# A decoder layer with 18 experts: rates and weights asked for earlier, two experts' products ahead, and the expert loops written out

## The chip, the cores and the metric

The kernel runs on one core of a Trainium2 chip. The core has five engines that run their own instruction streams and meet only at semaphores: TensorE (PE in the profile, matrix products), VectorE (DVE), ScalarE (ACT), GpSimd (POOL), and SyncE (SP), which here only issues DMAs. PSUM is eight banks of 128 x 512 floats; every product of TensorE lands there. The metric is the device time of one execution in microseconds (us), the median of several runs.

## What is computed

One decoder layer on `x` of 4 x 256 tokens with 256 features: a gated linear attention of 16 heads, a mixing of tokens by a softmax over a context, and an expert layer. Each has a layer norm ahead of it and is added to `x`. The change is in the second and the third.

```python
# mixing by context (query, key are bilinear maps of ctx_1024)
energy = einsum('bnd,bmd->bnm', query, key)
attention = softmax(energy, axis=-1)
x_m = einsum('bln,bmn->blm', x_norm, attention)
# experts: 2 shared (always used, weight 1) and 16 routed, 4 of them chosen per token
scores = sigmoid(hidden @ gate_weight.T)
#   two of four groups by their two best scores, then the four best experts, rates scaled to 2.5
y = sum over experts of  rate * ((silu(x @ gw.T) * (x @ uw.T)) @ dw.T)
```

## The kernel before, in words

All is one function, `decoder_layer`, with one instruction stream per engine, written by hand; the order of the work is the order of the code, and semaphore waits (`wait_ge`) hold an engine until another has got far enough. Every product of full precision is made of three (`mm3`, lines L1258 to L1260): both operands are split in a high and a low half, and high x low, low x high and high x high are added in PSUM. The high half is a copy on ScalarE, the low half a subtraction on VectorE or GpSimd.

The 16 heads fill the first 390 us and are not touched. Then comes a stretch in which the last head's output, the context softmax and the norms follow each other: ScalarE makes exponentials (`context_exp`, L685), scales them (`context_soft`, L693) and copies transposed tiles (`context_att`, `half_out`); VectorE adds into `x`, takes statistics and runs a chain of some 14 small operations for the norm's factors (`norm_factors`, L851 to L891); TensorE transposes (`half_transpose`, L1269) and mixes (`mix`, L1254). All of it goes in two halves of 512 tokens, `c` = 0 and 1.

The expert part has these pieces, `n` counting experts from 1 (1 and 2 are the shared ones, 3 to 18 the routed ones):
- `router_logits(c)` on TensorE, a sigmoid on ScalarE, a transpose, and then on VectorE a chain from L1179 to L1238 that chooses experts and makes the rates (`weight`, inside the tile `obet`). TensorE transposes the rates (L1646), ScalarE copies them, SP writes them to DRAM as rows (`route_rows`) and loads a row back for each expert, spread over all partitions (`load_route`, into `wbc`, the tile `tap`).
- `gate_up(n)` on TensorE: gate and up products of both halves, 24 matmuls of 512 columns into `e_ring` (banks 0 to 3).
- `gate_silu` (ScalarE, L777), `u_times` (VectorE, product of silu and up, L1149, into `prod`, the tile `conv`), `weigh` (GpSimd, times the rates, L502, into `act_w`, the tile `gate`), `act_high` (ScalarE, L786), `act_low` (VectorE, L1158): these make the two halves of the expert's activations.
- `down(n)` on TensorE: 24 matmuls of 256 columns, added up over all experts in `y_acc` (banks 4 to 7).
- Weights: SP loads 384 KB per expert into one of two slots of `w_raw`; ScalarE copies the high half (`gate_up_high` L761, `down_high` L768), GpSimd makes the low half (`gate_up_low` L484, `down_low` L490).

In before, TensorE multiplies one expert ahead: `gate_up(n + 1)` stands ahead of `down(n)`. The tiles of an expert's activations exist once. The shared experts are weighted on GpSimd too, by ones set with a memset (L508). Experts 5 to 18 run in a hardware loop of seven rounds of two on each engine (`Fori`).

Of the kernel before, what the change touches and what calls it, by code (L numbers as in the profile page):

```python
# [126 lines left out]
def decoder_layer(nc, x_in, ctx_in, xw_in, xb_in, wb_in, bb_in, w_in, prm_in, wv_in, wo_in,  # L127
# [5 lines left out]
    with ctx:  # L133
# [83 lines left out]
        mix_acc = bank[6:8] + bank[4:6]  # L217
        energy = (bank[0], bank[1], bank[0], bank[6])
# [10 lines left out]
        ld_w = [sem(f"ld_w{i}") for i in range(2)]  # L229
        ld_prm = [sem(f"ld_prm{i}") for i in range(G)]  # L230
# [29 lines left out]
        ones_ready = sem("ones_ready")  # L260
# [9 lines left out]
        def _(sp):  # L270
# [90 lines left out]
            def expert_split(n):  # L361


                sp.wait_ge(down_lo_ready, n - E_SHARED)


# [5 lines left out]
            load_expert(4, 1)  # L372
            sp.wait_ge(r_tr_ready, NCH)
# [3 lines left out]
            def load_route(e, s, before):  # L377

                sp.wait_ge(e_weighted, before)
# [17 lines left out]
        def _(pool):  # L397
# [89 lines left out]
            def down_low(n, s):  # L487
                w = slice(s * 3 * D + 2 * D, (s + 1) * 3 * D)
                pool.wait_ge(down_hi_ready, n - E_SHARED)
# [3 lines left out]
            def weigh(n, s, first):  # L493

                for c in range(NCH):
                    pool.wait_ge(u_prod, (n - 1) * NCH + c + 1)
                    if not first:

                        pool.wait_ge(e_hi, (n - 2) * NCH + c + 1)
                        pool.wait_ge(e_lo, (n - 2) * NCH + c + 1)  # L500
                    cc = slice(c * N, (c + 1) * N)
                    nc.gpsimd.tensor_tensor(act_w[:, cc], prod[:, cc], wbc[:, s * T + c * N:s * T + (c + 1) * N],  # L502
                                            ALU.mult).then_inc(e_weighted, 1)

            pool.wait_ge(p_added, TT // 2)
# [1211 lines left out]
```

## Time and profile before

| | |
|---|---|
| median of 3 runs | 598.84 us (596.99 to 599.95) |
| the profiled execution | 597.41 us |
| its span, first to last instruction | 595.5 us |
| PE busy | 557.4 us, 94% of the span |
| DVE / ACT / POOL busy | 437.1 / 398.3 / 298.9 us |
| chain that ended last | PE 83%, DVE 8%, ACT 4%, DMA 2% |

The span is shorter than the execution's own time by what lies ahead of the first and behind the last instruction. Matmuls overlap in the trace: a matmul of 512 columns is shown with some 0.39 us, but the next begins 0.23 us after it, so lengths of work on PE are taken from start to start. "Idle before" in a row is the time without work of that engine ahead of it, with the engine that ended it.

### The profile page before, as it was taken

How to read it: one execution, taken by the hardware profiler on the slowest of the kernel's cores; microseconds unless marked ns; L12 is line 12 of the kernel's file. 1: busy time of each engine (PE TensorE's matmuls, PEld its weight loads, DVE VectorE, ACT ScalarE, POOL GpSimd, SP SyncE). 2: the span in 40 equal slices, each digit the busy share in tenths (PEclk: the TensorE clock that was granted, in tenths of full speed). 3: DMA queues.
4: the chain of work that ended last, by engine and by line, in shares of the span. 5: the costliest groups of instructions: out<-in, count | busy, mean ns of one | idle time of the engine just before them, and what ended most of it. 6: DMA issues, size and time to landing. Idle time of an engine off the chain costs nothing.

```text
span 595.5 us, 10331 instructions
## 1 busy us (share of the span) xinstructions
PE 557.4 (94%) x3392; PEld 488.2 (82%) x3392; DVE 437.1 (73%) x1046; ACT 398.3 (67%) x783; POOL 298.9 (50%) x201
## 2 busy tenths in 40 slices
PE   3899999999999999999999999897777799999996
PEld 1687889989989989989989988786566688888885
DVE  8778989989989988998998998968593433333334
ACT  4978988878978979879779778665531433343331
POOL 2434756746746646656666563301041655556542
PEclk9998999999999999999999999999998899999999
DMA  6122032032032032032031020110002433333311
GB/s 206 29 107 81 0 117 81 1 116 81 2 117 81 2 116 81 2 116 75 8 116 56 27 97 23 59 29 1 0 1 70 149 105 107 104 123 113 108 62 70
DMA packets 16267, 42.23 MB, mean 71 GB/s; under 512 B 4544, under 2 KB 4800, under 8 KB 16224
## 3 DMA queue, kind: packets, MB, share of 16 engines
q1 hardware_dynamic: 16224, 41.69, 20.9%
q8 instruction: 23, 0.38, 0.3%
q14 instruction: 20, 0.16, 0.1%
HBM read 40.47 MB, written 1.21 MB: 70 GB/s over the span
## 4 chain that ended last, share of the span: by engine, by line
PE 83%; DVE 8%; ACT 4%; DMA 2%; issue 2%; SPq 1%; ACTq 0%; DVEq 0%
PE bank L1258 20%; PE bank L1260 19%; PE bank L1259 19%; PE bank L1254 15%; PE bank L1396 5%; PE bank L1384 4%; ACT tok L624 2%; DMA xbias<-in_xb 1%; DMA w_raw<-in_w 1%; DVE stats L976 1%; DVE xT_lo L911 1%; DVE gated_lo L1158 1%; ACT values L538 0%; DVE x L1248 0%; DVE raw L995 0%
## 5 line engine op out<-in xcount | busy, mean ns | idle before, releaser
L1258 PE MATMUL bank<-xT_lo,w_hi 128*128 128x512 f32 x336 | 140.0, 417 | 3.6 <-DVE conv L1149 1.3
L1260 PE MATMUL bank<-xT_hi,w_hi 128*128 128x512 f32 x336 | 132.3, 394 | 0.0
L1259 PE MATMUL bank<-xT_hi,w_lo 128*128 128x512 f32 x336 | 131.8, 392 | 0.0
L425 POOL TENSOR_TENSOR gated_lo<-gated,gated_hi 128x512 fp32r<-128x512 f32 x30 | 38.7, 1290 | 116.5 <-ACT gated_hi L644 112.8
L624 ACT ACTIVATE tok<-bank,nmr,rstd 128x128 f32<-128x128 f32 x256 | 91.0, 504 | 2.1 <-DVE nmr L891 2.1
L502 POOL TENSOR_TENSOR gate<-conv,tap 128x512 f32<-128x512 f32 x36 | 46.4, 1291 | 84.5 <-DVE conv L1149 71.4
L1258 PEld LDWEIGHTS bank<-xT_lo,w_hi 128*128 128x128 f32 x336 | 63.5, 189 | 18.8 <-DVE conv L995 3.2
L1260 PEld LDWEIGHTS bank<-xT_hi,w_hi 128*128 128x128 f32 x336 | 63.3, 188 | 14.2
L420 POOL TENSOR_TENSOR conv<-tap,conv 128x506 f32<-128x506 f32 x32 | 61.9, 1934 | 21.8 <-DVE conv L995 21.8
L420 POOL TENSOR_TENSOR raw<-tap,raw 128x506 f32<-128x506 f32 x32 | 61.9, 1934 | 20.3 <-DVE raw L995 16.3
L1259 PEld LDWEIGHTS bank<-xT_hi,w_lo 128*128 128x128 f32 x336 | 63.7, 190 | 9.6
L976 DVE BATCH_NORM_STATS2 stats<-bank 128x6 f32<-128x128 f32 x256 | 56.4, 283 | 16.3 <-PE bank L1384 16.3
L1149 DVE TENSOR_TENSOR conv<-bank,tok 128x512 f32<-128x512 f32 x36 | 24.8, 691 | 50.9 <-PE bank L1260 42.0
L967 DVE TENSOR_TENSOR_SCAN decay<-obet,dmask 128x1536 f32<-128x1536 f32 x16 | 61.9, 3868 | 0.0
L1158 DVE TENSOR_TENSOR gated_lo<-gate,gated_hi 128x512 fp32r<-128x512 f32 x36 | 25.5, 750 | 46.6 <-ACT gated_hi L786 46.6
L636 ACT ACTIVATE qk<-bank,prm 128x512 f32<-128x512 f32 x64 | 51.3, 840 | 0.0
L995 DVE SCALAR_TENSOR_TENSOR raw<-bank,prm,raw 128x510 f32<-128x510 f32 x64 | 46.8, 742 | 5.6 <-ACT tap L592 4.4
L1258 PE MATMUL bank<-w_lo,gated_hi 128*128 128x256 f32 x144 | 42.0, 292 | 9.3 <-DVE gated_lo L1158 9.3
L1254 PE MATMUL bank<-qk 128*128 128x256 f32 (+1 forms) x256 | 50.2, 329 | 0.5 <-DVE x L1028 0.3
L995 DVE SCALAR_TENSOR_TENSOR conv<-bank,prm,conv 128x510 f32<-128x510 f32 x64 | 46.8, 743 | 3.4 <-ACT tap L592 2.2
L1254 PEld LDWEIGHTS bank<-qk 128*128 128x128 f32 x256 | 43.3, 190 | 5.6 <-issue 0.7
L1254 PE MATMUL bank<-probs,values 128*128 128x256 f32 (+1 forms) x256 | 47.0, 327 | 0.0
(167 smaller groups left out, 1358.3 us busy)
## 6 DMA issues: line engine op xcount, KB each, us to landing
w_raw<-in_w SPq DMA_DIRECT2D x34, 384.0 KB, 4.4
obet<-obet_rows SPq DMA_DIRECT2D x16, 768.0 KB, 4.2
tap<-route_rows SPq DMA_DIRECT2D x16, 512.0 KB, 3.6
wv_raw<-in_wv SPq DMA_DIRECT2D x8, 256.0 KB, 4.8
wo_raw<-in_wo SPq DMA_DIRECT2D x8, 256.0 KB, 4.9
x<-in_x SPq DMA_DIRECT2D x2, 512.0 KB, 4.6
out_x<-x SPq DMA_DIRECT2D x4, 256.0 KB, 2.4
raw<-in_ctx SPq DMA_DIRECT2D x1, 512.0 KB, 5.4
```

Source lines behind the costliest of these rows:

```text
L420: nc.gpsimd.tensor_tensor(y, r, y, ALU.add).then_inc(conv_done, 1)
L425: nc.gpsimd.tensor_tensor(gated_lo[:, cc], gated[:, c * N:(c + 1) * N], gated_hi[:, cc].bitcast(F32), ALU.subtract).then_inc(gated_lo_read ...
L502: nc.gpsimd.tensor_tensor(act_w[:, cc], prod[:, cc], wbc[:, s * T + c * N:s * T + (c + 1) * N], ALU.mult).then_inc(e_weighted, 1)
L624: ins = nc.scalar.activation(tok[:, t * P:(t + 1) * P], t_ring[u][:, i * P:(i + 1) * P], ACT.Identity, scale=rstd[:, t:t + 1], bias=nmr[:, ...
L636: nc.scalar.activation(qk[:, u * N:(u + 1) * N], t_ring[u][:, :], ACT.Identity, scale=prm[:, o:o + 1], bias=prm[:, o + 1:o + 2]).then_inc( ...
L967: nc.vector.tensor_tensor_scan(decay[:, :], obet[:, :], dmask[:, :], 0.0, ALU.mult, ALU.add).then_inc(decay_ready, 1)
L976: ins = nc.vector.bn_stats(stats[:, 6 * t:6 * t + 6], t_ring[u][:, i * P:(i + 1) * P])
L995: ins = nc.vector.scalar_tensor_tensor(out=y, in0=r, scalar=prm[:, o + 3 - back:o + 4 - back], in1=y, op0=ALU.mult, op1=ALU.add)
L1254: return nc.tensor.matmul(o, l, r, start=start, stop=stop)
L1258: nc.tensor.matmul(o, l_hi, r_lo, start=start, stop=False, skip_group_check=loose)
L1259: nc.tensor.matmul(o, l_lo, r_hi, start=False, stop=False, skip_group_check=loose)
L1260: return nc.tensor.matmul(o, l_hi, r_hi, start=False, stop=stop, skip_group_check=loose)
```

## The change

Nothing is computed otherwise but this: the shared experts are no longer multiplied by ones. The rest moves work or gives it room:
- Weights of experts 3 and 4 are split early, whole, into the tiles of the attention's weights (`early`: `wv_hi`/`wv_lo`, `wo_hi`/`wo_lo`), which are free by then; ScalarE does it ahead of the second `context_soft`, GpSimd after the first mixed quarter is added to `x`.
- Every tile on an expert's way exists twice (`two`, `weighted`), so TensorE multiplies two experts ahead: `gate_up(n + 2)` ahead of `down(n)`.
- Shared expert 2's first half uses banks 6 and 7 (`e_bank`); the two shared experts are interleaved by halves and parts (`e_count` gives their order). `mix`, norm and router are reordered at this place: the transposes of the router's first half come after three of four mixed quarters, and the second pair of exponentials after the first `half_out`.
- Weight loads are split in gate and up (256 KB) and down (128 KB), and rows of rates are asked for an expert earlier.
- GpSimd makes the next gate weights' low half between its two weightings.
- The loops on all five engines are written out.

```diff
-        act_w = gate
-        act_hi, act_lo = gated_hi[:, 0:T], gated_lo[:, 0:T]
+        act_hi, act_lo = gated_hi[:, 0:2 * T], gated_lo[:, 0:2 * T]
...
+        def two(n, c):
+            return slice(n % 2 * T + c * N, n % 2 * T + (c + 1) * N)
+        def e_bank(n, c, j):
+            return bank[6 + j] if isinstance(n, int) and n == 2 and c == 0 else e_ring[2 * c + j]
+        def e_count(n, c):
+            if isinstance(n, int) and n <= E_SHARED:
+                return n + E_SHARED * c
+            return n * NCH + (c + 1 - NCH)
+        def weighted(n, c):
+            if n <= E_SHARED:
+                return prod[:, two(n, c)]
+            o = n % 2 * 3 * T + c * N
+            return gate[:, o:o + N]
+        def early(n):
+            return (wv_hi[:, 64:64 + 3 * D], wv_lo[:, 64:64 + 3 * D]) if n == 3 else (
+                wo_hi[:, 0:3 * D], wo_lo[:, 0:3 * D])
...
-        mix_acc = bank[6:8] + bank[4:6]
-        energy = (bank[0], bank[1], bank[0], bank[6])
+        mix_acc = bank[4:8]
+        energy = (bank[0], bank[1], bank[6], bank[7])
```

SyncE:

```diff
-            for s in range(2):
-                load_route(s, s, NCH * (s + 1))
-            with sp.Fori(0, E_ROUTED // 2 - 1) as r:
+            for e in range(3):
+                load_route(e, e % 2)
+            for r in range(E_ROUTED // 2 - 2):
                 for s in range(2):
-                    expert_split(r * 2 + (3 + s))
-                    load_expert(r * 2 + (5 + s), s)
-                    load_route(r * 2 + (2 + s), s, r * (2 * NCH) + NCH * (3 + s))
+                    load_gate_up(r * 2 + (7 + s), s)
+                    load_route(r * 2 + (3 + s), 1 - s)
+                    load_down(r * 2 + (7 + s), s)
+            load_route(E_ROUTED - 1, 1)
```

GpSimd:

```diff
-            pool.wait_ge(p_added, TT // 2)
-            nc.gpsimd.memset(wbc, 1.0).then_inc(ones_ready, 1)
-            pool.wait_ge(ones_ready, 1)
-            weigh(1, 0, True)
-            gate_up_low(3, 0)
-            weigh(2, 1, False)
-            gate_up_low(4, 1)
-            down_low(3, 0)
+            pool.wait_ge(x_mixed, 1)
+            early_low(3)
+            early_low(4)
+            pool.wait_ge(r_ready, 1)
+            gate_up_low(5, 0)
+            gate_up_low(6, 1)
+            def step(n, m, s, up=True, down=True):
+                pool.wait_ge(ld_route[s], n * 8 - (1 + s) * 8)
+                weigh(n, m, s, 0)
+                if up:
+                    gate_up_low(n + 1, 1 - s)
+                weigh(n, m, s, 1)
+                if down:
+                    down_low(n, s)
...
-            with pool.Fori(0, E_ROUTED // 2 - 1) as r:
+            for r in range(E_ROUTED // 2 - 3):
```

ScalarE:

```diff
             context_soft(0)
-            context_exp((4, 5))
             context_att(0)
             half_norm(1, 0)
+            half_out(1, 0, xT)
+            context_exp((4, 5))
             context_exp((6, 7))
-            half_out(1, 0, xT)
+            early_high(3)
+            early_high(4)
             context_soft(1)
...
+            def step(n, m, s, up=True):
+                gate_silu(n, m)
+                if up:
+                    gate_up_high(n + 1, 1 - s)
+                act_high(n, m)
+                down_high(n, s)
```

TensorE (the transposes of the rates stand where `r_ready` is waited for):

```diff
-            mix(1)
+            mix(1, (2,))
+            half_transpose(2, 0)
+            mix(1, (3,))
...
             router_logits(0)
-            gate_up(1, 0, True, (0,))
+            gate_up(1, 0, ((0, 0), (0, 1)))
+            gate_up(2, 1, ((0, 0),))
             half_transpose(2, 1)
+            gate_up(2, 1, ((0, 1),))
             pe.wait_ge(ln_split, 2 * KT * NCH)
             router_logits(1)
-            gate_up(1, 0, True, (1,))
+            gate_up(1, 0, ((1, 0),))
...
-            gate_up(2, 1)
+            gate_up(1, 0, ((1, 1),))
             pe.wait_ge(r_tok_ready, 1)
-            down(1, 0, True, False)
-            gate_up(3, 0, chunks=(0,))
-            down(2, 1, False, False)
+            down(1, 1, 0, (0,))
+            gate_up(2, 1, ((1, 0), (1, 1)))
+            down(1, 1, 0, (1,))
+            gate_up(3, 0)
+            down(2, 2, 1, (0,))
             pe.wait_ge(r_ready, 1)
...
+            down(2, 2, 1, (1,))
             pe.wait_ge(r_tr_ready, NCH)
-            gate_up(3, 0, chunks=(1,))
             gate_up(4, 1)
-            down(3, 0, False, False)
-            with pe.Fori(0, E_ROUTED // 2 - 1) as r:
+            gate_up(5, 0)
+            down(3, 3, 0)
+            gate_up(6, 1)
+            down(4, 4, 1)
+            for r in range(E_ROUTED // 2 - 2):
                 for s in range(2):
-                    gate_up(r * 2 + (5 + s), s)
-                    down(r * 2 + (4 + s), 1 - s, False, False)
-            down(E_ALL, 1, False, True)
+                    gate_up(r * 2 + (7 + s), s)
+                    down(r * 2 + (5 + s), 5 + s, s)
+            down(E_ALL - 1, E_ALL - 1, 0)
+            down(E_ALL, E_ALL, 1)
```

How the instructions stand, at three places. GpSimd between the last head and the first routed expert, before; `gate<-conv,tap0` is a weighting, `w_lo<-w_raw,w_hi` a low half of weights:

```order
L425 TENSOR_TENSOR gated_lo<-gated,gated_hi 128x512 [waits gated_hi_ready]
L508 MEMSET tap0 128x2048 [waits p_added]
L502 TENSOR_TENSOR gate<-conv,tap0 128x512 [waits u_prod,ones_ready]
L502 TENSOR_TENSOR gate<-conv,tap0 128x512 [waits u_prod]
L484 TENSOR_TENSOR w_lo<-w_raw,w_hi 128x512 [waits w_hi_ready]
L502 TENSOR_TENSOR gate<-conv,tap0 128x512 [waits e_lo,e_hi,u_prod] x2
L484 TENSOR_TENSOR w_lo<-w_raw,w_hi 128x512 [waits w_hi_ready]
L490 TENSOR_TENSOR w_lo<-w_raw,w_hi 128x256 [waits down_hi_ready]
```

The same place of the change:

```order
L464 TENSOR_TENSOR gated_lo<-gated,gated_hi 128x512 [waits gated_hi_ready]
L536 TENSOR_TENSOR wv_lo<-w_raw,wv_hi 128x768 [waits w_hi_ready,x_mixed]
L536 TENSOR_TENSOR wo_lo<-w_raw,wo_hi 128x768 [waits w_hi_ready]
L523 TENSOR_TENSOR w_lo<-w_raw,w_hi 128x512 [waits w_hi_ready,r_ready]
L523 TENSOR_TENSOR w_lo<-w_raw,w_hi 128x512 [waits w_hi_ready]
L546 TENSOR_TENSOR gate<-conv,tap0 128x512 [waits u_prod,ld_route0]
```

The two early subtractions stand first, released by the first mixed quarter (`x_mixed`), and the next work waits for the finished rates (`r_ready`); the weightings of the shared experts are gone.

ScalarE from the first softmax scaling to the second, before (`qk<-bank` is `half_out`, `gate,small<-bank` an exponential):

```order
L693 ACTIVATE gate<-gate,small 128x256 x3
L685 ACTIVATE gate,small<-bank0,small 128x256 [waits x_max] x2
L699 ACTIVATE attT<-bank0 128x512 [waits x_attT_full]
L699 ACTIVATE attT<-bank1 128x512 [waits x_attT_full]
L538 ACTIVATE values<-x,nmr,rstd 128x256 [waits ln_rstd]
L538 ACTIVATE values<-x,nmr,rstd 128x256
L685 ACTIVATE gate,small<-bank6,small 128x256 [waits x_max] x2
L546 ACTIVATE qk<-bank0 128x512 [waits ln_full]
L546 ACTIVATE qk<-bank1 128x512 [waits ln_full]
L693 ACTIVATE gate<-gate,small 128x256 [waits x_recip]
```

The same stretch of the change:

```order
L740 ACTIVATE gate<-gate,small 128x256 x3
L746 ACTIVATE attT<-bank0 128x512 [waits x_attT_full]
L746 ACTIVATE attT<-bank1 128x512 [waits x_attT_full]
L585 ACTIVATE values<-x,nmr,rstd 128x256 [waits ln_rstd]
L585 ACTIVATE values<-x,nmr,rstd 128x256
L593 ACTIVATE qk<-bank0 128x512 [waits ln_full]
L593 ACTIVATE qk<-bank1 128x512 [waits ln_full]
L732 ACTIVATE gate,small<-bank6,small 128x256 [waits x_max] x2
L732 ACTIVATE gate,small<-bank7,small 128x256 [waits x_max] x2
L811 ACTIVATE wv_hi<-w_raw 128x768 [waits c_full,ld_w0]
L811 ACTIVATE wo_hi<-w_raw 128x768 [waits p_full,ld_w1]
L740 ACTIVATE gate<-gate,small 128x256 [waits x_recip]
```

Exponentials moved behind the copies of the normed input, and two copies of weights stand ahead of the second scaling.

TensorE around the transposes of the rates (`bank2<-ident,obet`), before; what follows them is the second half of expert 3's gate products (`xT_lo,w_hi`), waiting for ScalarE's copy of the rates:

```order
L1260 MATMUL bank7<-w_hi,gated_hi 128x256
L1646 MATMUL bank2<-ident,obet 16x128 [waits u_prod,g_silu,r_ready]
L1646 MATMUL bank2<-ident,obet 16x128 x3
L1646 MATMUL bank3<-ident,obet 16x128 x4
L1258 MATMUL bank2<-xT_lo,w_hi 128x512 [waits g_silu,w_lo_ready,r_tr_ready]
```

And of the change:

```order
L1348 MATMUL bank5<-w_hi,gated_hi 128x256
L1751 MATMUL bank2<-ident,obet 16x128 [waits u_prod,g_silu,r_ready]
L1751 MATMUL bank2<-ident,obet 16x128 x3
L1751 MATMUL bank3<-ident,obet 16x128 x4
L1346 MATMUL bank6<-w_lo,gated_hi 128x256 [waits e_lo]
```

Behind the transposes now stand down products of expert 2 (banks 6 and 7), which do not wait for ScalarE's copy.

## Rows read from the trace of the kernel before

**Rows 1.** The page, part 1: busy us, share of the span, instructions.

```profile
PE 557.4 (94%) x3392; PEld 488.2 (82%) x3392; DVE 437.1 (73%) x1046; ACT 398.3 (67%) x783; POOL 298.9 (50%) x201
```

**Rows 2.** Table of stretches, router to loop, and loop.

```profile
core 0: us, PE busy (x) PEld busy (x) DVE busy (x) ACT busy (x) POOL busy (x), PEclk, DMA share, GB/s
...
419.97:471.32 51.35, 40.11 (x204) 32.41 (x205) 28.23 (x75) 17.67 (x31) 15.73 (x13) 0.93 0.14 48
471.32:587.17 115.85, 115.85 (x674) 102.25 (x672) 38.47 (x56) 43.83 (x83) 66.60 (x55) 1.00 0.31 100
```

**Rows 3.** TensorE's waits from 400 to 596: us in total, times, longest.

```profile
PE bank L1258 <- DVE gated_lo L1158: 9.3, 4, 3.2
PE bank L1258 <- DVE xT_lo L911: 4.1, 2, 2.5
...
PE bank L1258 <- DVE conv L1149: 1.3, 1, 1.3
PE bank L1258 <- ACT gate L823: 0.7, 1, 0.7
```

**Rows 4.** Timeline of TensorE: start us, us shown, what, idle before.

```profile
419.97 0.40 PE L1258 MATMUL bank<-xT_lo,wv_hi 128*16 128x512 f32 x1 [2.54 <-DVE xT_lo L911]
...
450.19 0.42 PE L1258 MATMUL bank<-w_lo,gated_hi 128*128 128x256 f32 x1
...
467.02 0.55 PE L1258 MATMUL bank<-w_lo,gated_hi 128*128 128x256 f32 x1 [3.16 <-DVE gated_lo L1158]
...
471.32 0.40 PE L1258 MATMUL bank<-xT_lo,w_hi 128*128 128x512 f32 x1
...
578.89 0.40 PE L1258 MATMUL bank<-xT_lo,w_hi 128*128 128x512 f32 x1
...
584.37 0.28 PE L1258 MATMUL bank<-w_lo,gated_hi 128*128 128x256 f32 x1
...
588.93 0.36 PE L1258 MATMUL bank<-w_lo,gated_hi 128*128 128x256 f32 x1 [1.60 <-DVE gated_lo L1158]
```

**Rows 5.** Timeline of VectorE in the router's chain.

```profile
431.96 1.22 DVE L1179 TENSOR_TENSOR obet<-obet 128x128 f32<-128x128 f32 x1 [0.37 <-ACT obet L811]
...
436.22 0.18 DVE L1204 TENSOR_SCALAR obet<-obet 128x32 f32<-128x32 f32 x1
...
437.05 0.28 DVE L1209 TENSOR_TENSOR obet<-obet 128x128 f32<-128x128 f32 x1
437.36 1.17 DVE L1210 TENSOR_SCALAR obet<-obet 128x32 f32<-128x32 f32 x1
...
447.67 0.70 DVE L1229 TENSOR_TENSOR raw<-raw 128x128 f32<-128x128 f32 x1
...
450.90 0.29 DVE L1238 TENSOR_TENSOR obet<-obet 128x128 f32<-128x128 f32 x1
```

**Rows 6.** Timeline of GpSimd.

```profile
437.21 1.29 POOL L502 TENSOR_TENSOR gate<-conv,tap 128x512 f32<-128x512 f32 x1 [4.18 <-DVE conv L1149]
...
461.27 2.54 POOL L502 TENSOR_TENSOR gate<-conv,tap 128x512 f32<-128x512 f32 x2 [13.06 <-DMA tap<-route_rows]
```

**Rows 7.** Timeline of SyncE: issue of the rates' DMA.

```profile
455.34 0.34 SPq L374 DMA_DIRECT2D route_rows<-gate  x1
```

**Rows 8.** Stretch before the router, and the forms that it gains.

```profile
405.37 1.70 ACT L693 ACTIVATE gate<-gate,small 128x256 f32<-128x256 f32 x4 [0.73 <-DVE small L946]
...
L685 ACT ACTIVATE gate<-bank,small 128x256 f32<-128x256 f32 x8 | 3.7, 468 | 0.4 <-DVE small L940 0.3
...
L566 ACT ACTIVATE w_hi<-w_raw x18: 837/841/872, 9.9 to 373.7; 128x768 fp32r<-128x768 f32 x18
...
L405 POOL TENSOR_TENSOR w_lo<-w_raw,w_hi x18: 1818/1850/1933, 10.9 to 375.1; 128x768 fp32r<-128x768 f32 x18
...
410.98 0.17 DVE L851 TENSOR_TENSOR nw<-stats 128x4 f32<-128x4 f32 x1
...
413.36 0.73 DVE L902 TENSOR_SCALAR values<-x,rstd,nmr 128x256 f32<-128x256 f32 x2
...
412.83 3.72 PE L1254 MATMUL bank<-attT,qk 128*128 128x256 f32 x16 [0.74 <-ACT qk L546]
```

More of the change, by code:

```diff
@@ L229, in decoder_layer @@
         ld_w = [sem(f"ld_w{i}") for i in range(2)]
+        ld_down = [sem(f"ld_down{i}") for i in range(2)]
         ld_prm = [sem(f"ld_prm{i}") for i in range(G)]
@@ L488, in down_low @@
                 w = slice(s * 3 * D + 2 * D, (s + 1) * 3 * D)
-                pool.wait_ge(down_hi_ready, n - E_SHARED)
+                pool.wait_ge(down_hi_ready, n - 4)
                 nc.gpsimd.tensor_tensor(w_lo[:, w], w_raw[:, w], w_hi[:, w].bitcast(F32),
                                         ALU.subtract).then_inc(down_lo_ready, 1)
[L493 to L503, printed above, removed]
@@ L1162, in by_tile, with act_low @@
+            def act_low(n, m, chunks=range(NCH)):
+                for c in chunks:
+                    dve.wait_ge(e_hi, n * NCH + (c + 1 - NCH))
+                    nc.vector.tensor_tensor(act_lo[:, two(m, c)], weighted(m, c),
+                                            act_hi[:, two(m, c)].bitcast(F32),
+                                            ALU.subtract).then_inc(e_lo, 1)
+            u_times(1, 1, (0,))
+            half_low(2, 1)
+            u_times(2, 2, (0,))
             def by_tile(ap):
@@ L1603, in down @@
-            def down(n, s, first, last):
-                if not (isinstance(n, int) and n <= E_SHARED):
-                    pe.wait_ge(down_lo_ready, n - E_SHARED)
-                o = s * 3 * D + 2 * D
-                for t in range(TT):
-                    if t % G == 0:
-                        pe.wait_ge(e_lo, (n - 1) * NCH + t // G + 1)
-                    tt = slice(t * P, (t + 1) * P)
-                    ins = mm3(y_acc[t // 2][:, (t % 2) * D:(t % 2 + 1) * D], act_hi[:, tt], act_lo[:, tt],
-                              w_hi[:, o:o + D], w_lo[:, o:o + D], first and t % 2 == 0, last, loose=True)
-                    if last and t % 2:
-                        ins.then_inc(y_full, 1)
-                if not last:
-                    ins.then_inc(e_down, 1)
@@ L1620, in _ @@
-            half_transpose(2, 0)
+                hi, lo = w_hi[:, s * 3 * D:(s + 1) * 3 * D], w_lo[:, s * 3 * D:(s + 1) * 3 * D]
+                if isinstance(n, int) and n in (3, 4):
+                    hi, lo = early(n)
+                for c, j in parts:
+                    if isinstance(n, int) and n == 2 and c == 0:
+                        pe.wait_ge(x_mixed, TT // 2)
+                    elif not (isinstance(n, int) and n == 1):
+                        pe.wait_ge(g_silu if j == 0 else u_prod, e_count(n - 1, c))
+                    for kt in range(KT):
+                        o = j * D + kt * P
+                        ins = mm3(e_bank(n, c, j)[:, :], hi[:, o:o + P], lo[:, o:o + P],
+                                  xs_(xT_hi, kt, c * N, (c + 1) * N), xs_(xT_lo, kt, c * N, (c + 1) * N),
+                                  kt == 0, kt == KT - 1)
+                    ins.then_inc(e_full, 1)
@@ new lines, in down @@
+            def down(n, m, s, chunks=range(NCH)):
+                hi, lo = w_hi[:, s * 3 * D:(s + 1) * 3 * D], w_lo[:, s * 3 * D:(s + 1) * 3 * D]
+                if m in (3, 4):
+                    hi, lo = early(m)
+                elif m > 4:
+                    pe.wait_ge(down_lo_ready, n - 4)
+                o = 2 * D
+                for c in chunks:
+                    if m == 1 and c == 1:
+                        pe.wait_ge(u_prod, e_count(2, 0))
+                    pe.wait_ge(e_lo, n * NCH + (c + 1 - NCH))
+                    for t in range(G * c, G * (c + 1)):
+                        tt = slice(m % 2 * T + t * P, m % 2 * T + (t + 1) * P)
+                        ins = mm3(y_acc[t // 2][:, (t % 2) * D:(t % 2 + 1) * D], act_hi[:, tt], act_lo[:, tt],
+                                  hi[:, o:o + D], lo[:, o:o + D], m == 1 and t % 2 == 0, m == E_ALL, loose=True)
+                        if m == E_ALL and t % 2:
+                            ins.then_inc(y_full, 1)
+                    if m < E_ALL and c == NCH - 1:
+                        ins.then_inc(e_down, 1)
```

253 lines of the change are left out of this document (145 added, 108 removed).

## The prediction

> **What bounds the kernel now.** The page's busy shares come first: TensorE works 94% of the span [rows 1], so a gain must come from its remaining idle time or from its clock. The table of two stretches then says where that time lies. From the router's first product (419.97) to the first product of the old loop (471.32) TensorE is busy 40.11 of 51.35 us at a granted clock of 0.93; from there to 587.17 it is busy all 115.85 us at 1.00 [rows 2]. The loops are therefore paced by matmuls alone: the first group at 471.32 and that of the last expert at 578.89 are 13 experts apart, 8.275 us each, of which the gate and up products take 584.37 - 578.89 = 5.48 and the down products the other 2.80 [rows 4]. The list of TensorE's waits names the holes around the loops: 9.3 us in four waits for the low half of an expert's activations (L1158), 4.1 in two for the low half of the normed input (L911), 1.3 for a product (L1149), 0.7 for the transposed rates (L823) [rows 3]; one of the first kind, 1.60 us, stands at the very end [rows 4].
>
> The price of the holes is more than these waits. Work between the first router product (419.97) and the last down group (588.93) is 18 x 5.48 + 17 x 2.80 + two router products of 1.4 + 2.4 for 24 transposes, 151.4 us; it took 168.96. So 17.5 us are lost: 1.6 (of the 4.1, the 2.5 stand ahead of 419.97) + 1.3 + 9.3 + 0.7 = 12.9 of waits [rows 3, 4], some 3.1 of half clock after two of them (a matmul of 256 columns then takes 0.42 us; the down group from 467.02 to 471.32 took 4.30 instead of 2.80, [rows 4]; clock 0.93 in [rows 2]), the rest restarts after a wait.
>
> **The router's chain on VectorE is slowed by GpSimd.** From L1179 (431.96) to L1238 (ends 451.19) the chain that makes the rates takes 19.2 us, and TensorE's transposes of the rates wait for it. In it an operation with constants on 128x32 takes 1.17 us where the same form a few lines earlier takes 0.18 [rows 5]; it ends at 438.53, just after a GpSimd multiply that began at 437.21 ends (438.50) [rows 6]. Seven operations, the first L1179 (1.22), the last L1229 (0.70), are stretched so; against 0.28 for an undisturbed one of 128x128 [rows 5] that is 5.8 us.
>
> **The change, part by part.**
> Before the experts: nothing up to 391.8 is touched. From there ScalarE has the second pair of exponentials later and two copies more (weights of experts 3 and 4, 128x768, 0.84 each as in [rows 8]). The input's halves are copied until about 404.25, four exponentials at some 0.46 follow to 406.0, the copies to 407.5, so the second softmax scaling starts at 407.5 instead of 405.37 [rows 8]. The transposes, copies and mixing products behind it come 1.0 us later (413.8 against 412.83 [rows 8]). Against that, the transposes for the router's first half now stand after three quarters of the mixing, not after all of it: alone worth 1.3 us.
> But GpSimd's two subtractions for these copies (1.85 each, [rows 8]) start once the first mixed quarter is added, about 410.1, and run to 413.75, over the norm chain of VectorE (2.4 us from L851 to L902, [rows 8]). Most of its operations read two SBUF tensors, as the stretched L1229 of [rows 5] does, so I let them wait for the second subtraction: the chain ends at 416.1 instead of 414.2, and the router's first product starts at 419.95, as before. Bounds: 418.7 if nothing collides; 421.0 if the four statistics ahead of the chain are held up too, which no row shows. The Trainium skill (SBUF — State Buffer, section "SBUF: two separate sides") says that VectorE takes the port shared with GpSimd when an instruction has two SBUF inputs or runs in a two-port mode, and that the loser is blocked for the whole instruction. By it the chain waits and the statistics with one input pass, which gives 582.4 below; the rows alone leave 581.1 to 583.5.
>
> Shared experts 1 and 2: their weighting by ones on GpSimd is gone (four multiplies of 1.29) and so are the three subtractions of weights that ran in the chain's time; GpSimd has nothing to do from 413.8 until the rates are ready. I take all 5.8 us off the chain, and 1.2 for two expert operations that now stand ahead of it. It starts about 431.8 (the score's copy on ScalarE still ends there: one table load and one copy stand ahead of it, but the second half's transposes come earlier) and ends at 431.8 + 19.2 - 7.0 = 444.0 instead of 451.19.
> TensorE meanwhile has more to do ahead of it: products of expert 2's first half run in two spare banks, expert 3's weights are ready, so 3 can be multiplied whole. Following its new order with the durations above: router 1 at 428.0 (a hole of 0.35), expert 1's second half, down 1 to 434.2, half of expert 2, a hole of 0.75 for the product of expert 1 (its VectorE multiply sits in the chain at 435.4), down 1's second half at 437.75, gate and up of 3 from 439.15 to 444.6, down 2's first half to 446.0. Rates (444.0) and expert 3's product (445.4) are there by then, so the transposes start at 446.0, not 453.6; down 2's second half covers ScalarE's copy, and expert 4 starts at 448.35. The four waits of [rows 3] between 437 and 467 shrink to these two holes of 1.1 us together.
>
> The old 3.16 us wait was for expert 3's rates: the rows leave by DMA at 455.34 [rows 7] and GpSimd's first weighting starts at 461.27 [rows 6], 5.9 us later. Now the same trip starts at 447.75, weighting at 453.7 and done at 456.2, high and low halves by 458.2 to 458.9; TensorE has experts 4 and 5 to multiply (2 x 5.48) and reaches down 3 at 459.3. Cover: 0.4 to 1.1 us; without it the wait is back in part.
>
> Experts 5 to 18: same matmuls, so 8.275 each. Down n now follows the products of n + 2, so its halves have 16.5 us instead of 5.5. Tightest is the low half of the next gate weights: gate products of the second half end 4.1 us into a group, then 0.6 for silu, 0.63 for the copy, 1.29 for GpSimd and 0.3 of hand-overs give 7.0, and the next group starts at 8.28: 1.25 spare. Loads are split in two (256 and 128 KB) and asked for a whole expert ahead. At the end down 17 fills the last 1.60 us.
> The loops' removal I cost at nothing, in both directions: 24 matmuls at 0.2275 and 24 at 0.117 are 8.27, so the 8.275 us of the 13 looped experts leave no room for a jump's cost, and the stretch before 391.8 was written out already.
>
> **Sum.** Expert 4 at 448.35, then 15 x 5.48 + 15 x 2.80 = 124.2 to the last down group: 572.55, against 588.93. The 6.57 us from there to the end (595.5) stay. Span 579.1, 16.4 less. The profiled execution took 597.41 with a span of 595.5; the median of the runs is 598.84, 1.4 above it. 598.84 - 16.4 = 582.4 us, a gain of 2.7%. Its own range is 579 to 585: 418.7 and no hole give 2.4 less, a late start of the router and a hole at down 3 give up to 2 more, and the three runs of before spread over 3 us.
>
> **Rivals.**
> 1. The chain's long operations are slow of themselves and not held by GpSimd: then it ends at about 449.8, down 1's second half starts at 440.5, expert 4 only at 453.5: 5.2 us more, 587.6, and 589 with another stretch at half clock. For it: some of the seven have forms found nowhere else. Against: two of equal form in neighbouring lines differ sixfold [rows 5]. Chance 0.12.
> 2. The first routed experts still starve: rates or weights of 5 and 6 land later than the old trip says, since three loads of rates and expert 7's weights follow each other on one DMA queue. The old wait of 3.16 and its 1.5 of half clock come back: 587. Chance 0.14.
> 3. Slower than before: the 1.25 us spare of the next gate weights is not there, because GpSimd does its two weightings of 1.29 first or waits for VectorE, in each of the 12 steps. It decides from 1.4 us of loss a step (16.8 us), that is when the low half comes 2.65 us later than reckoned; at 1.7 a step (20.4 us) the time is 603. The new order puts the subtraction between the two weightings, which speaks against it. Chance 0.03.
> 4. No change: the gain at the experts is taken by a longer stretch before the router, 598. It would take 16 us where I find 1 to 2. Chance 0.02.
> My forecast has 0.69. Range 578 to 589.5, which takes in rivals 1 and 2. What a measurement of this kernel can tell from no change is about 0.5%, 3 us: faster 0.95, same 0.02, slower 0.03.
>
> **What would show it.** Right: TensorE busy without a hole from about 448 to the last adds; no operation of the rates' chain over 0.9 us, the chain about 12 us long; transposes of the rates near 446; clock 1.00 throughout; no wait at the last down group. Wrong: norm operations after 411 stretched by more than 2 us, a wait at down 3 or at the gate products of 7 and 8, or a period over 8.3 us.

## The result, and the profile after

The changed kernel takes 581.67 us (median of 4 runs, 580.70 to 582.77) against 597.91 for the kernel before: a ratio of 0.973, 95% interval 0.968 to 0.978. Forecast were 582.4. The profiled execution took 582.77 us with a span of 581.0, 14.5 less than before; forecast was a span of 579.1. So the median came out within 0.8 us and the span 1.9 us off; where the 1.9 lie is the question of most experiments below.

The page of the changed kernel first: busy time of each engine, and TensorE's busy share and granted clock in 40 slices of 14.5 us.

```profile
PE 556.8 (96%) x3392; PEld 487.5 (84%) x3392; DVE 433.4 (75%) x1046; ACT 398.3 (69%) x782; POOL 292.8 (50%) x194
...
PE   3898999999999999999999999989799999999997
...
PEclk9998999999999999999999999999799999999999
```

TensorE does the same work (556.8 us against 557.4 in [rows 1]) in a shorter span. The clock has two dents: an 8 in the fourth slice and a 7 in the 29th, at 406 to 421. The next view is the table of two stretches: router to experts, and experts, as in [rows 2]; the last columns are clock, DMA share and GB/s.

```profile
421.34:472.26 50.92, 50.49 (x278) 41.48 (x277) 30.90 (x86) 22.01 (x38) 16.49 (x12) 1.00 0.20 66
472.26:580.00 107.74, 105.20 (x626) 93.30 (x624) 36.18 (x54) 37.67 (x74) 57.82 (x48) 1.00 0.31 102
```

In before TensorE was busy 40.11 of 51.35 us after the router's first product, at clock 0.93. Now it is busy 50.49 of 50.92, at 1.00: the holes among the first experts are gone, and in nearly the same time the stretch holds the gate and up products of two more experts and the down products of one more. The list of TensorE's waits, from 400 to the end (total, times, longest), says what remains of [rows 3]:

```profile
PE bank L1357 <- ACT values L585: 1.7, 1, 1.7
PE bank L1342 <- DVE x L1187: 1.2, 1, 1.2
PE bank L1401 <- ACT gate L740: 0.7, 1, 0.7
PE bank L1342 <- ACT qk L593: 0.7, 1, 0.7
PE bank L1346 <- DVE conv L1226: 0.2, 1, 0.2
PE bank L1346 <- DVE xT_lo L986: 0.2, 1, 0.2
```

The first four, 4.3 us, all stand ahead of the router, and behind it 0.4 us are left. No wait for an expert's activations (9.3 us in [rows 3]) is in the list. The timeline of TensorE ahead of the router, and three of its later starts (start, us, engine, line; idle time before in brackets):

```profile
404.80 3.69 PE L1342 MATMUL bank<-attT,qk 128*128 128x256 f32 x16 [1.17 <-DVE x L1187]
409.24 1.10 PE L1401 MATMUL bank<-ident,gate 128*128 128x128 f32 x8 [0.75 <-ACT gate L740]
412.05 1.94 PE L1357 MATMUL bank<-ident,values 128*128 128x128 f32 x8 [1.71 <-ACT values L585]
414.67 3.78 PE L1342 MATMUL bank<-attT,qk 128*128 128x256 f32 x8 [0.69 <-ACT qk L593]
418.24 1.39 PE L1357 MATMUL bank<-ident,values 128*128 128x128 f32 x8
...
421.34 0.41 PE L1346 MATMUL bank<-xT_lo,wv_hi 128*16 128x512 f32 x1
...
450.01 0.39 PE L1346 MATMUL bank<-xT_lo,wo_hi 128*128 128x512 f32 x1
...
461.05 0.28 PE L1346 MATMUL bank<-wv_lo,gated_hi 128*128 128x256 f32 x1
...
574.40 0.38 PE L1346 MATMUL bank<-w_lo,gated_hi 128*128 128x256 f32 x1
```

Here lies the miss. Eight mixing products take 3.78 us at 414.67; sixteen of the same form took 3.69 at 404.80. The clock fell at the transposes of 412.05 (1.94 instead of 1.10), after two idle pieces of 0.75 and 1.71 us. The transposes lose 0.8 us by it and the mixing 1.9, but TensorE would have waited for the norm chain for a part of that (experiment 4): the router starts at 421.34 instead of 419.95, 1.4 later. From there to expert 4 (450.01) it is 28.67 us (forecast 28.40), and from there to the last down group (574.40) 124.4 (forecast 124.2). VectorE, the head of the norm chain and three rows of the rates' chain, with GpSimd's three that matter:

```profile
410.63 1.39 DVE L971 BATCH_NORM_STATS2 stats<-x 128x6 f32<-128x256 f32 x4
412.06 1.73 DVE L926 TENSOR_TENSOR nw<-stats 128x4 f32<-128x4 f32 x1
413.72 0.15 DVE L927 TENSOR_TENSOR nw<-stats 128x4 f32<-128x4 f32 x1
...
433.38 0.29 DVE L1260 TENSOR_TENSOR obet<-obet 128x128 f32<-128x128 f32 x1 [2.49 <-ACT obet L881]
...
437.85 0.18 DVE L1291 TENSOR_SCALAR obet<-obet 128x32 f32<-128x32 f32 x1
...
445.26 0.29 DVE L1318 TENSOR_TENSOR obet<-obet 128x128 f32<-128x128 f32 x1
```

```profile
410.20 1.81 POOL L536 TENSOR_TENSOR wv_lo<-w_raw,wv_hi 128x768 fp32r<-128x768 f32 x1 [19.21 <-DVE x L1187]
411.96 1.81 POOL L536 TENSOR_TENSOR wo_lo<-w_raw,wo_hi 128x768 fp32r<-128x768 f32 x1
...
455.59 5.95 POOL L546 TENSOR_TENSOR gate<-conv,tap 128x512 f32<-128x512 f32 x4 [6.69 <-DMA tap<-route_rows]
```

The rates' chain runs from 433.38 to 445.55, 12.17 us as forecast (19.2 in [rows 5]); L1291, once L1210 with 1.17, takes 0.18. In the norm chain only the first operation is stretched, to 1.73, and ends with GpSimd's second subtraction; the four statistics ahead of it are not held up.

### The profile page after: what moved, and what is told of

It is laid out like the page before. It is cut to its first block, busy times and chain, and to the rows that moved or that the text cites. A ratio compares the mean times of both kernels' runs of the same rounds, so it can differ in the third digit from the quotient of the medians.

```text
span 581.0 us, 9944 instructions
## 1 busy us (share of the span) xinstructions
PE 556.8 (96%) x3392; PEld 487.5 (84%) x3392; DVE 433.4 (75%) x1046; ACT 398.3 (69%) x782; POOL 292.8 (50%) x194
## 4 chain that ended last, share of the span: by engine, by line
PE 88%; ACT 4%; DVE 4%; issue 1%; DMA 1%; SPq 0%; DVEq 0%; ACTq 0%
PE bank L1346 21%; PE bank L1348 20%; PE bank L1347 20%; PE bank L1342 16%; PE bank L1483 5%; PE bank L1471 4%; ACT tok L671 2%; DMA xbias<-in_xb 1%; DVE stats L1051 1%; PE bank L1357 1%; PE bank L1550 1%; ACT values L585 1%; DVE x L1336 0%; DVE raw L1070 0%; DVE xT_lo L986 0%
## 5 line engine op out<-in xcount | busy, mean ns | idle before, releaser
L1346 PE MATMUL bank<-xT_lo,w_hi 128*128 128x512 f32 x320 | 133.7, 418 | 1.9 <-DVE conv L1070 1.2
L1348 PE MATMUL bank<-xT_hi,w_hi 128*128 128x512 f32 x320 | 126.1, 394 | 0.0
L1347 PE MATMUL bank<-xT_hi,w_lo 128*128 128x512 f32 x320 | 125.6, 392 | 0.0
L1346 PEld LDWEIGHTS bank<-xT_lo,w_hi 128*128 128x128 f32 x320 | 60.5, 189 | 16.1 <-DVE conv L1070 3.2
L1348 PEld LDWEIGHTS bank<-xT_hi,w_hi 128*128 128x128 f32 x320 | 60.3, 189 | 13.5
L1347 PEld LDWEIGHTS bank<-xT_hi,w_lo 128*128 128x128 f32 x320 | 60.7, 190 | 9.1
L546 POOL TENSOR_TENSOR gate<-conv,tap 128x512 f32<-128x512 f32 x32 | 42.7, 1340 | 20.5 <-DVE conv L1226 13.2
L1234 DVE TENSOR_TENSOR gated_lo<-gate,gated_hi 128x512 fp32r<-128x512 f32 x32 | 23.6, 775 | 38.9 <-ACT gated_hi L849 38.6
L849 ACT ACTIVATE gated_hi<-gate 128x512 fp32r<-128x512 f32 x32 | 18.8, 626 | 46.7 <-PE bank L1348 43.0
```

What stands on the lines that cost most here:

```text
L546: nc.gpsimd.tensor_tensor(weighted(m, c), prod[:, two(m, c)], wbc[:, s * T + c * N:s * T + (c + 1) * N], ALU.mult).then_inc(e_weighted, 1)
L1346: nc.tensor.matmul(o, l_hi, r_lo, start=start, stop=False, skip_group_check=loose)
L1347: nc.tensor.matmul(o, l_lo, r_hi, start=False, stop=False, skip_group_check=loose)
L1348: return nc.tensor.matmul(o, l_hi, r_hi, start=False, stop=stop, skip_group_check=loose)
```

## The experiments

Ratios are to the kernel before; the changed kernel has 0.973 [0.968, 0.978] and, in a second series, 0.972 [0.968, 0.976]. In single executions the span depends on where the clock fell, so spans are given with the mean clock.

**1. Loops back.** All five engines get their loops again:

```diff
-            for r in range(E_ROUTED // 2 - 2):
+            with pe.Fori(0, E_ROUTED // 2 - 2) as r:
```

> The changed kernel with one part undone: the last loops stand in Fori loops again on all five engines, the order of the work is the same. Theory (the loops' removal is worth nothing): span 581.0 +- 0.3, 8.275 us from one expert's first gate product to the next, within 0.1% of the changed kernel. Rival (a jump or the fetching of a loop's code costs TensorE time, or delays the engine that feeds it): each of the six rounds longer than 16.55 us, span 582 or more.

Measured: 582.52 us median of 6, ratio 0.974 [0.970, 0.978], profiled span 580.8. Two of its rounds of two experts in its table of stretches, and the same two in that of the changed kernel:

```profile
471.97:488.52 16.55, 16.55 (x98) 14.63 (x98) 5.36 (x8) 6.26 (x12) 9.68 (x8) 1.00 0.35 112
488.52:505.07 16.55, 16.55 (x98) 14.62 (x97) 5.36 (x8) 6.27 (x12) 9.68 (x8) 1.00 0.35 111
```

```profile
472.26:488.81 16.55, 16.55 (x99) 14.63 (x98) 5.36 (x8) 6.12 (x12) 9.68 (x8) 1.00 0.33 112
488.81:505.36 16.55, 16.55 (x99) 14.62 (x98) 5.35 (x8) 6.12 (x12) 9.67 (x8) 1.00 0.34 112
```

TensorE fills every round to the end in both, 16.55 us, so writing the loops out is worth nothing here. The Trainium skill (Advanced Engine Details and Errata, section "Control Flow Timing") gives about 108 ns for a compare-and-branch; no row here shows such a time on TensorE's path.

**2. One expert ahead again.**

```diff
             gate_up(4, 1)
-            gate_up(5, 0)
             down(3, 3, 0)
-            gate_up(6, 1)
+            gate_up(5, 0)
             down(4, 4, 1)
+            gate_up(6, 1)
+            down(5, 5, 0)
```

and in the loop `down` of n - 1 instead of n - 2.

> The changed kernel with one part undone: TensorE multiplies one expert ahead again (the products of n + 1, then down n); earlier rates, early weights and double tiles stay. Theory (the second expert ahead covers the trip of the rates): down 3 would start at 455.6, but its activations are ready only at about 460.4; a hole of some 5 us, some 1.5 of half clock behind it, and about 1.8 again at the end: span 589 to 590, period 8.275. Rival (earlier weights and rates alone took the old waits away): only the hole at the end, span 582.8.

Measured: 589.55 us, ratio 0.989 [0.983, 0.995], span 587.6. TensorE's waits behind the router in its list:

```profile
PE bank L1346 <- DVE gated_lo L1234: 4.5, 2, 3.1
...
PE bank L1346 <- POOL w_lo L529: 1.7, 1, 1.7
```

The hole at down 3 is there, but 3.08 us and not 5, since its first half needs only the first half's activations (I had counted to the second's). Another of 1.38 at down 4 was not expected. Down 3 takes 4.42 us instead of 2.80, the second half of it at half clock, and 1.70 come back at the end, there for GpSimd's low half of the down weights. That makes 7.8 us. From the router's first product to the end it is 168.3 us (from 419.32 to 587.6) instead of 159.7, 8.6 more; the other 0.8 I put down to the restarts after the holes. The medians differ by 7.9, or by 8.7 from the second series of the changed kernel. The rival, that earlier rates and weights alone removed the waits, falls.

**3. GpSimd back in the rates' chain.** Eight multiplies of dead tiles, one after the other:

```diff
+            pool.wait_ge(r_tok_ready, 1)
+            for i in range(8):
+                nc.gpsimd.tensor_tensor(probs[:, 0:N], decay[:, 0:N], dmask[:, 0:N], ALU.mult).then_inc(dum, 1)
+                pool.wait_ge(dum, i + 1)
             pool.wait_ge(r_ready, 1)
```

> The changed kernel with eight multiplies of 128x512 on GpSimd added while VectorE makes the rates; they read and write tiles that nobody uses any more, so only GpSimd's use of SBUF changes. Theory (GpSimd's multiplies hold up VectorE's small operations): operations of the chain take up to 1.2 us again, the chain takes 18 to 20 us instead of 12.2, TensorE waits for the rates, span 587 to 590. Rival (the old chain was long of itself, or the shared experts' weighting was what it waited for): chain 12.2 us, span 581 to 581.5.

Measured: 589.24 us, ratio 0.986 [0.981, 0.991]; three spans of 587.3 to 587.5 at clock 0.991, and the profiled one of 590.1 at 0.982. VectorE's timeline (line numbers six higher than in the changed kernel), and GpSimd's row beside it:

```profile
433.15 1.19 DVE L1271 TENSOR_TENSOR obet<-obet 128x32 f32<-128x32 f32 x1
434.27 0.21 DVE L1272 TENSOR_TENSOR obet<-obet 128x32 f32<-128x32 f32 x1
434.40 1.32 DVE L1273 TENSOR_TENSOR obet<-obet 128x32 f32<-128x32 f32 x1
...
452.33 0.29 DVE L1324 TENSOR_TENSOR obet<-obet 128x128 f32<-128x128 f32 x1
```

```profile
432.87 11.05 POOL L558 TENSOR_TENSOR probs<-decay,dmask 128x512 f32<-128x512 f32 x8 [19.49 <-ACT obet L887]
```

The chain takes 19.8 us, and TensorE waits 7.9 us in one piece for a product that stands in it. Equal operations in neighbouring lines differ sixfold again, with nothing but these multiplies added. Together with the 12.17 us of the changed kernel this refutes rival 1 of the prediction: the old chain was not long of itself. Nor did it wait for the weighting of the shared experts: from 431.96 to 451.19 VectorE's timeline of before has no idle time.

**4. Memsets in the same place,** eight of 128x1024, which read no SBUF:

```diff
-                nc.gpsimd.tensor_tensor(probs[:, 0:N], decay[:, 0:N], dmask[:, 0:N], ALU.mult).then_inc(dum, 1)
+                nc.gpsimd.memset(probs[:, 0:2 * N], 1.0).then_inc(dum, 1)
```

> As the kernel with eight GpSimd multiplies in the rates' chain, but with eight memsets of 128x1024, which write SBUF and read nothing. Theory (the blocked side is the path on which GpSimd reads): the chain stays at 12.2 us and the span at 581.0 +- 0.4. Rival (any long GpSimd operation on SBUF blocks VectorE): the chain is stretched as with the multiplies, span over 585.

Measured: 582.17 us, ratio 0.975 [0.969, 0.980]. GpSimd is busy 8.08 us in the chain, which takes 12.7. One of VectorE's operations is longer; its row, and GpSimd's:

```profile
433.45 0.72 DVE L1291 TENSOR_SCALAR obet<-obet 128x32 f32<-128x32 f32 x1
```

```profile
430.15 8.08 POOL L558 MEMSET probs<- 128x1024 f32 x8 [18.17 <-ACT obet L887]
```

All operations with two SBUF operands pass. One with a single operand and constants (L1291 here is L1285 of the changed kernel, where it takes 0.18) takes 0.72 and ends at 434.17, where the fourth memset ends (430.15 + 4 x 1.01). The Trainium skill (SBUF — State Buffer, section "SBUF: two separate sides") says just this of both kinds: two SBUF inputs collide only with a GpSimd operation that reads SBUF, VectorE's two-port modes with any. The first the trace bears out; that L1291 runs in such a mode is a guess from its one operand, which no run here shows. The next operation of its form, L1297, takes 0.18, but at 435.13, just as the fifth memset ends, so it says nothing either way.

This execution shows something else too. Up to the router it is the changed kernel, but its clock did not fall there:

```profile
403.01 3.69 PE L1348 MATMUL bank<-attT,qk 128*128 128x256 f32 x16 [1.17 <-DVE x L1193]
...
410.25 1.09 PE L1363 MATMUL bank<-ident,values 128*128 128x128 f32 x8 [1.71 <-ACT values L591]
412.08 1.99 PE L1348 MATMUL bank<-attT,qk 128*128 128x256 f32 x8 [0.74 <-ACT qk L599]
...
418.10 0.40 PE L1352 MATMUL bank<-xT_lo,wv_hi 128*16 128x512 f32 x1
```

With equal holes ahead (0.74 and 1.71 us), the transposes take 1.09 and the mixing 1.99. The router starts 15.1 us after the first mixing product (403.01), not 16.5. The forecast, 419.95 with that product at 404.80, is 15.15.

**5. The changed kernel again.**

> The changed kernel itself once more, as the base for the three kernels beside it. From the spans so far (581.0, 580.8, 579.0, 578.9 at a mean clock of 0.991 to 0.994) theory (half clock falls by chance in two places, 1.7 us within the first 50 us and 1.4 to 1.9 ahead of the router): the six executions spread from 577.8 with neither to 581.1 with both, in steps. Rival (the spread is noise of another kind): executions lie evenly and the mean clock does not order them.

Its ten executions of both series, with the mean clock: four spans of 580.5 to 581.0 at 0.990 or 0.991, five of 578.9 to 579.1 at 0.993 or 0.994, one of 577.6 at 0.999. They lie in steps, as expected. The profiled one of 578.9 has clock 1.00 in the first 50 us (0.97 in the one of 581.0) and 0.84 from 403 to 424. By these steps the half clock ahead of the router came in nine of ten, and another, in the heads, in four of ten. Span and clock together tell the two apart: with the one in the heads alone, as in experiment 6, the span is 579.1 to 579.2 too, but the mean clock 0.996 or 0.997.

Nine of ten is not the whole record, for other kernels here have the same two holes. Of seven traces with them six show the fall; the memset kernel's does not. By span and clock, two of that kernel's four executions kept the clock there (578.3 at 0.999, 579.6 at 0.997), and two of four in the first kernel of experiment 7: with these, 13 of 18 fell. The six executions with loops do not all fit the steps (580.8 at 0.995, 578.8 at 0.996) and are left out.

**6. Filling the holes.** Products that nobody reads, ahead of and behind the transposes at 412.05:

```diff
+            pe.wait_ge(x_exp, TT)
+            def warm():
+                for _ in range(3):
+                    mm(bank[7][:, 0:D], qctx[:, 0:P], kctx[:, 0:D], True, True)
+            warm()
             half_transpose(1, 1)
+            warm()
             mix(1, (2,))
```

A first form had six of 128x512 a time.

> The changed kernel with twelve products of 128x512 that nobody uses added on TensorE, six in each of the two holes around the transposes at 412.05, into a bank that is written afresh afterwards; nothing else changes. Theory (the holes let the clock fall, and that is the missing 1.4 us): clock 1.00 from 409 to 419, the mixing quarter at 414.67 takes 1.9 instead of 3.78, the next start is set by the norm chain's end at 416.0, and the router's first product comes at 419.9, span 579.6. Rival (the clock falls whatever TensorE does there, or the norm chain's end sets the start already): router's first product at 421.3, span 581.0.

That form missed its aim by my sizing: 586.33 us, span 583.9. The operands are no split halves but plain f32, and each product shows as two rows 0.43 us apart, 5.3 us for six where I had 1.4. The clock did stay at 1.00 and the mixing took 1.89, but the filling outlasted the holes. Of two such kernels the second had GpSimd's subtractions later as well, and is void for the same reason (587.43 us):

> Both edits: the added products keep TensorE busy, and GpSimd's subtractions come after the norm. Theory (two limits of nearly the same time lie over each other, the half clock and the blocked chain): together they give what neither gives alone, router's first product at 418.2 to 418.7 and span 578.0 to 578.6. Rival (a third thing sets the start, such as ScalarE's half of the norm): not before 419.5, span 579.3 or more.

The form shown above has three of 128x256:

> The changed kernel with three unused products of 128x256 (1.3 us) in each of the two holes around the transposes at 412.05, in place of the six of 128x512 that turned out to take 5.2 us each time. Theory (the holes let the clock fall, and that is the missing 1.4 us): clock 1.00 from 405 to 424 in every execution; router's first product 15.1 us after the first mixing product (404.80 in the changed kernel, so 419.9 by its time) instead of 16.5; spans 579.6 with the half clock of the first 50 us, 577.9 without it. Rival (the clock falls there all the same, or the added products delay the work): 16.5 us or more, spans up to 581.

Its timeline:

```profile
404.47 3.69 PE L1342 MATMUL bank<-attT,qk 128*128 128x256 f32 x16 [1.17 <-DVE x L1187]
...
411.72 1.10 PE L1357 MATMUL bank<-ident,values 128*128 128x128 f32 x8 [0.41 <-ACT values L585]
412.65 1.46 PE L1342 MATMUL bank<-attT 128*128 128x256 f32 x6
413.95 1.89 PE L1342 MATMUL bank<-attT,qk 128*128 128x256 f32 x8
416.82 1.09 PE L1357 MATMUL bank<-ident,values 128*128 128x128 f32 x8 [0.99 <-ACT values L585]
...
419.56 0.40 PE L1346 MATMUL bank<-xT_lo,wv_hi 128*16 128x512 f32 x1
```

The router starts 15.09 us after the first mixing product, and the wait of 0.99 shows what sets it now: the norm that follows the blocked chain. Six spans: 577.7 and 577.8 at 0.999 and 1.000, four of 579.1 to 579.2 at 0.996 or 0.997. By these steps the half clock at this place is gone in six of six; with the four other kernels that have filled holes (here and below), in 24 of 24, none of them under 0.996. The median is no better (580.93 us, ratio 0.971 [0.967, 0.975]), since the other one, in the heads, came in four of the six.

**7. GpSimd's early subtractions behind the norm,** alone and with the filled holes:

```diff
-            pool.wait_ge(x_mixed, 1)
+            pool.wait_ge(ln_norm_dve, 2 * 3 * NCH)
             early_low(3)
```

> The changed kernel with GpSimd's two early subtractions (weights of experts 3 and 4) put off until VectorE has normed its part of the second half ahead of the router. Theory (the half clock, not the blocked norm chain, sets the router's first product): the chain's first operation takes 0.15 instead of 1.73 us and the chain ends 1.7 earlier, at 414.3, but TensorE mixes at half clock until 418.2 all the same: router's first product 421.0 to 421.4, span within 0.4 of 581.0. Rival (the collision sets the router's start): 419.6, span 579.3.

> The same added products, and GpSimd's two early subtractions put off until VectorE has normed its part. Theory (without half clock the blocked norm chain sets the router's start): 1.7 us more, router's first product 13.4 us after the first mixing product, spans 577.9 with the half clock of the first 50 us and 576.2 without. Rival (something else sets it): 14.5 us or more.

Alone:

```profile
404.23 3.69 PE L1342 MATMUL bank<-attT,qk 128*128 128x256 f32 x16 [1.17 <-DVE x L1187]
...
414.12 3.72 PE L1342 MATMUL bank<-attT,qk 128*128 128x256 f32 x8 [0.69 <-ACT qk L593]
...
420.74 0.40 PE L1346 MATMUL bank<-xT_lo,wv_hi 128*16 128x512 f32 x1 [0.29 <-DVE xT_lo L986]
```

```profile
411.50 0.17 DVE L926 TENSOR_TENSOR nw<-stats 128x4 f32<-128x4 f32 x1
```

L926 takes 0.17 instead of 1.73, but in the profiled execution the clock falls as before, and the router starts 16.51 us after the first mixing product against 16.54; span 580.4. Half clock covers the collision whole. Where the clock did not fall, two executions had spans of 576.4 and 576.6, 1.0 to 1.2 less than the changed kernel's 577.6. The median is 579.69, ratio 0.969 [0.964, 0.974]. With filled holes the router starts after 14.25 us, 0.84 less than with the holes filled alone; 13.4 was expected and 14.5 the rival's. TensorE there waits 0.29 for `xT_lo` (L986), which on VectorE stands behind the next quarter's addition and statistics: that is the limit behind the blocked norm. All four spans are 578.2 to 578.5 at 0.997, median 580.07.

**8. ScalarE's early copies later too,** behind `half_out(2, 0)`:

```diff
-            early_high(3)
-            early_high(4)
             context_soft(1)
...
             half_out(2, 0, xT_hi)
+            early_high(3)
+            early_high(4)
```

> The changed kernel with GpSimd's early subtractions after the norm and ScalarE's two early copies of weights after the second layer's first half is copied out, where nothing waits for them at once. Theory (the copies' 1.5 us ahead of the second softmax scaling make the holes): scaling at 406.0 instead of 407.47, the hole of 0.75 gone, no half clock, router's first product 418.0 to 418.7, span 577.7 to 578.4, about 579 us by the clock of the runs. Rival (the copies then hold up what follows them on ScalarE, the first silu or the normed second half, or the clock falls all the same): span 580 or more.

> Added products, GpSimd's subtractions after the norm and ScalarE's early copies after the second layer's first half: all of what the experiments point to. Theory: as with the subtractions alone, less 0.7 to 1.4 for the second softmax scaling that no longer waits for the copies; spans 575.2 to 577.2, the median about 577.5 us in the clock of the runs. Rival (the added products overrun the shorter holes and take the gain back): spans 576.5 to 578.5.

Both kernels keep the edit of experiment 7. Without filling: the hole of 0.75 is gone, 578.00 us median of 7 (577.83 to 581.57), ratio 0.968 [0.964, 0.971]. Five of the seven executions have clock 1.00 throughout and spans of 576.0 to 576.2. In the profiled one the clock fell after all, at the mixing of 412.66; span 579.8. With filling the router starts after 13.51 us, 0.74 less again; all six executions had the half clock in the heads (0.996 or 0.997), spans 577.3 to 577.6, median 579.34. That is above the theory's 577.2 and inside the rival's range. Less the 1.4 us of the heads by the steps of experiment 6 it would be some 576.1 (an estimate), what the unfilled form has when its clock holds, so filling as well gains nothing more there. The unfilled form is the fastest that ran. Against the changed kernel at 577.6 with clock 0.999 it gains 1.5 us at full clock; the intervals of the two ratios still overlap.

## Why the prediction was right, and where it was off

- **The rates' chain (7.0 us off it)**: held to 0.03 us, and experiment 3 shows the cause.
- **Shared experts and expert 3**: holes of 0.2 and 0.24 us where 0.35 and 0.75 were forecast. Rival 1 did not come.
- **The trip of the rates**: 6.1 us from the rows' DMA (449.45) to the first weighting (455.59), forecast 5.9. Both low halves of expert 3 are ready at 460.39, down 3 starts at 461.05 without a wait: a cover of 0.66, forecast 0.4 to 1.1. Rival 2 did not come, and experiment 2 shows that the second expert ahead is what prevents it.
- **Experts 5 to 18**: 8.275 us each. GpSimd has the next gate weights 1.56 us early at expert 7 (forecast 1.25), so rival 3 has no ground. Loops at nothing: experiment 1.
- **The step that was mis-sized: the stretch ahead of the router**, "the router's first product starts at 419.95, as before". It came at 421.34. The ends named on the way were right (second scaling 407.47, chain's end 416.0), as were the collision of VectorE and GpSimd and the passing statistics. What I left out was the clock: the forecast had "clock 1.00 throughout", since in before holes of like size left it at full speed (clock of the mixing at 412.83 by its length, [rows 8]). It had not counted that the change adds a hole: in before the transposes at 408.25 follow the mixing without a pause, now TensorE waits 0.75 us for the second scaling, which the forecast itself put 2.1 us later. Without this hole (experiment 8, unfilled) one execution of seven fell. Experiments 4 and 6 show 15.1 us, the forecast's value, when the clock holds, and 5 that it mostly does not. That is 1.4 of the 1.9 us by which the span was off; 0.5 are small terms.
- The collision was priced at 1.25 us of the router's start (419.95 against 418.7). Experiment 7 gives 0.84 with filled holes, 1.0 to 1.2 by spans at full clock without them, and nothing under half clock.
- The close median owes something to luck. Counted from the profiled execution of before, 597.41 - 16.4 = 581.0 was forecast and the profiled one of the change took 582.77, 1.8 more. But the sum went on top of 598.84, the median of three. The spans of 33 further executions of before lie between 591.7 and 599.2 with the middle at 595.4, about 597.3 in time (1.9 more, as in the profiled one), so the base was some 1.5 us high. And the profiled execution of the change has both half clocks; the median of its four lies 1.1 below it. These two hide the miss.

Two parts of the change carry most of it: undoing the second expert ahead alone, or putting GpSimd back in the chain alone, each costs some 8 us. The second is more than the change itself took off, since the eight multiplies stretch the chain by 7.6 us and the work of before by 5.8, and the two can overlap. What the early weights, the split loads and the spare banks are worth by themselves no run here shows. What stays open too is why the same code, with the same holes, keeps the clock in one execution and loses it in another.

## What to carry to other kernels

When a chain of small VectorE operations sets the pace, look at what GpSimd does beside it: equal operations with sixfold different times, ending with a GpSimd row, are the mark, and the cure here was to move GpSimd's reads elsewhere. A second unit of work in flight paid here because the way from the rates' DMA to finished activations (10.9 us, 449.45 to 460.39) is longer than the gate and up products of one expert (5.48); its price was only buffers. Where TensorE has several holes close together, price the work behind them at either clock, and run a kernel several times before a microsecond is put down to a cause.

## What the runs showed of the hardware that I had not expected

Two idle pieces of 0.75 and 1.71 us with 1.1 us of transposes between them cost the full clock in six of seven traces, and by span and clock in 13 of 18 executions; the others kept it. With 1.3 us of products in each hole it stayed in six of six, and in 24 of 24 executions of all kernels with filled holes. Under half clock a later limit disappears (0.84 us of collision were worth nothing). GpSimd memsets, 8.08 us of them, cost the chain of VectorE 0.53 us, multiplies of 11.05 us cost it 7.6.
